# First pair's banks, VectorE order and load order of an attention and expert kernel changed, and the last keys' product as three half-precision passes

## The reference

```
x = x + xattn(layernorm(x), ctx)     # queries from x, keys and values from the context
x = x + attn(layernorm(x))           # 16 heads, rotated queries and keys
x = x + ffn(layernorm(x))            # 8 experts, the best 2 of each token

# xattn, after a second layernorm of the queries and one of the context:
q = x1 @ Wq + bq;  k = x2 @ Wk + bk;  v = x2 @ Wv + bv
attn = softmax(q @ k.T * scaling)    # 32 queries by 257 keys in each batch
y = (attn @ v) @ Wo + bo
```

## Time and profile before

| | |
|---|---|
| median of 3 runs | 574.69 us |
| the profiled execution | 574.39 us |
| its span, first to last instruction | 572.1 us |
| TensorE busy | 488.4 us, 85% |
| VectorE busy | 381.2 us, 67% |
| ScalarE busy | 253.2 us, 44% |
| GpSimd busy | 111.0 us, 19% |
| mean granted TensorE clock | 0.930 |

### The profile page before, as it was taken

The page is one execution under the profiler, slowest core; times in us unless marked ns, Lnnn a source line. Parts: engine busy times, 40 slices in busy tenths (PEclk is TensorE's granted clock), DMA queues, the critical chain, the costliest instruction groups (busy, mean ns, idle before and its releaser), DMA issues.

```text
span 572.1 us, 11023 instructions
## 1 busy us (share of the span) xinstructions
PE 488.4 (85%) x3598; PEld 277.6 (49%) x3599; DVE 381.2 (67%) x850; ACT 253.2 (44%) x392; POOL 111.0 (19%) x88
## 2 busy tenths in 40 slices
PE   4988699998988999859503799999999999999993
PEld 2743266465665777636401344544454445444441
DVE  4776878848979898878785566673655636673230
ACT  1403346465269293948400445652545526542130
POOL 1030122114150222102750011112111211121112
PEclk9979699999999999995655799999999999999998
DMA  8997087920009993361596468787584866734222
GB/s 297 405 391 288 32 340 302 406 103 1 1 2 384 379 383 126 111 220 38 186 320 183 124 198 231 253 233 221 155 255 78 269 168 197 222 77 74 55 55 38
DMA packets 56128, 111.56 MB, mean 195 GB/s; under 512 B 25216, under 2 KB 26272, under 8 KB 50976
## 3 DMA queue, kind: packets, MB, share of 16 engines
q1 hardware_dynamic: 25152, 87.64, 42.2%
q10 hardware_dynamic: 26640, 13.73, 10.0%
q0 software_dynamic: 4304, 9.77, 7.9%
HBM read 76.19 MB, written 29.43 MB: 185 GB/s over the span
## 4 chain that ended last, share of the span: by engine, by line
PE 63%; DVE 15%; DMA 8%; issue 5%; POOL 4%; ACT 2%; SPq 2%; ACTq 0%; POOLq 0%; DVEq 0%
PE bank L716 20%; PE bank L734 19%; PE bank L536 6%; PE bank L355 4%; DMA wbuf<-in_wo 4%; POOL routed_rows L1673 3%; DMA ctx_region<-in_ctx 2%; PE bank L520 2%; PE bank L562 2%; PE bank L427 2%; PE bank L501 2%; PE bank L613 1%; DMA routed_rows<-shared,ints 1%; DVE ctx_region L1324 1%; PE bank L496 1%
## 5 line engine op out<-in xcount | busy, mean ns | idle before, releaser
L716 PE MATMUL bank<-wbuf,ctx_region 128*128 x504 | 116.4, 389 | 6.5 <-issue 5.4
L1458 DVE SCALAR_TENSOR_TENSOR wbuf<-ctx_region,wbuf 128x2048 f32 (+1 forms) x28 | 62.9, 2288 | 32.5 <-ACT wbuf L900 32.5
L1703 POOL DMA_INDIRECT out<-misc,ints x21 | 38.6, 1838 | 229.6 <-ACT misc L981 174.6
L716 PEld LDWEIGHTS bank<-wbuf,ctx_region 128*128 128x128 f16 x504 | 49.0, 100 | 66.0 <-issue 13.9
L900 ACT ACTIVATE wbuf<-ctx_region 128x2048 f32 (+1 forms) x28 | 52.0, 1903 | 29.1 <-issue 29.1
L1608 POOL TENSOR_TENSOR small<-small 128x2 f32<-128x2 f32 (+2 forms) x25 | 27.1, 1088 | 171.4 <-DVE small L1054 160.1
L734 PE MATMUL bank<-wbuf,actT 128*128 x264 | 58.8, 379 | 1.0 <-DVE actT L1568 1.0
L1000 ACT ACTIVATE ctxT_region<-bank 128x512 f32<-128x512 f32 x42 | 25.1, 597 | 67.8 <-PE bank L716 67.8
L734 PE MATMUL bank<-wbuf,xn 128*128 x240 | 53.4, 379 | 0.0
L536 PE MATMUL bank<-ctx_region,wbuf 128*128 128x256 f16 x384 | 43.3, 273 | 3.7 <-DVE ctx_region L1209 3.7
L1562 DVE CAST ctxT_region<-ctxT_region 128x1024 f16<-128x1024 f32 x21 | 14.6, 694 | 42.9 <-ACT ctxT_region L1000 42.9
(11 more groups left out here) (220 smaller groups left out, 790.6 us busy)
## 6 DMA issues: line engine op xcount, KB each, us to landing
ctx_region<-in_experts SPq DMA_DIRECT2D x28, 1024.0 KB
routed_rows<-ctxT_region SPq DMA_DIRECT2D x1, 16900.0 KB, 50.7
ctxT_region<-in_ctxT SPq DMA_DIRECT2D x8, 1542.0 KB, 13.2
ctx_region<-in_ctx SPq DMA_DIRECT2D x8, 1536.0 KB, 10.2
ctx_region<-routed_rows ACTq DMA_DIRECT2D x23, 260.0 KB, 4.0
wbuf<-in_experts SPq DMA_DIRECT2D x4, 1024.0 KB
out<-x ACTq DMA_DIRECT2D x8, 256.0 KB
wbuf<-in_wqT SPq DMA_DIRECT2D x4, 256.0 KB, 7.3
```

What stands on the lines that cost most here:

```text
L716: mm = nc.tensor.matmul(bank[half][:, :], xgT[:, b, x_part, k * P:(k + 1) * P], w16[:, ds(at + (w_part + k * EH + half * 512), 512)], star ...
L1458: nc.vector.scalar_tensor_tensor(w16[:, ds(at + (LOW + n * PIECE), PIECE)], src_[:, piece], W_SCALE, w16[:, ds(at + (HIGH + n * PIECE), PI ...
L1703: nc.gpsimd.indirect_dma_start(out, bass.IndirectOffsetOnAxis(idx[:, slot_no:slot_no + 1].bitcast(U32), axis=0), y_out[:, slot_no, :], Non ...
```

## The change

It has four parts.

1. Banks and waits of pair 0. The third product of `join_values` goes to bank 3 instead of bank 0 and waits for `sc_nb` (tile 1's scores have been read). `join_biases` goes to bank 5 instead of bank 1 and waits for `left_bias` instead of `r_out`. The wait for `m2_lo` moves from between `probs_T` and `queries_T` to ahead of tile 1 of `context_sums`, the wait for `bvo` to ahead of `probs_T`.
2. VectorE's order in pair 0: the first half of `ctx_stats(2)`, `query_second(1)` and `query_shift(1)` now stand ahead of `context_max(0)`, the third `values_low` and `query_stats(2)` behind `probs_scaled(0)`.
3. Load order: `wvT` and `wo` now come ahead of `load_ctx(1)`. At the start the first x tiles come behind `wkT` of block 1, and the semaphores are cut anew, so that `fold(e)` no longer waits for `wqT` of its own block and TensorE's block e waits for `wqT` of its block.
4. The left keys' product is three half-precision passes (high by high, high by low, low by high) behind the other keys, instead of one float32 matmul ahead of them. VectorE makes the two halves of the left rows once (`left16`) and one more half of `p_left` per tile.

```diff
-            sp.dma_start(ln2_rows, t_in["ln2_rows"]).then_inc(s["ln2_in"], 16)
+            sp.dma_start(ln2_rows, t_in["ln2_rows"]).then_inc(qk_in[0], 16)
             for e in range(KC):
                 part = slice(e * P, (e + 1) * P)
                 sp.dma_start(wkT[:, e, :], t_in["wkT"][part, :]).then_inc(qk_in[e], 16)
-                sp.dma_start(wqT[:, e, :], t_in["wqT"][part, :]).then_inc(qk_in[e], 16)
-                if e == 0:
+                if e == 1:
                     sp.dma_start(x_tiles[:, 0:2], x_dram[:, 0:2]).then_inc(s["x_in0"], 16)
+                sp.dma_start(wqT[:, e, :], t_in["wqT"][part, :]).then_inc(qk_in[e + 1], 16)
...
             load_ctxT(1)
-            load_ctx(1)
             sp.dma_start(left_row[0:B, :], t_in["ctx_768"][:, KEYS - 1, :]).then_inc(s["left_in"], 16)
             load_w(wvT, "wvT", s["vo_weights_in"])
             load_w(wo, "wo", s["vo_weights_in"])
+            load_ctx(1)
...
-                pe.wait_ge(qk_in[e], 32)
+                pe.wait_ge(qk_in[e + 1], 32 if e + 1 < KC else 16)
...
                         join_biases()
+                        pe.wait_ge(s["sc_nb"], 2)
                     for e in range(KC):
-                        mm = nc.tensor.matmul(bank[(6, 7, 0)[k]][:, :], wvT[:, e, k * P:(k + 1) * P], wo[:, e, :],
+                        mm = nc.tensor.matmul(bank[(6, 7, 3)[k]][:, :], wvT[:, e, k * P:(k + 1) * P], wo[:, e, :],
                                               start=(e == 0), stop=(e == KC - 1))
...
-                pe.wait_ge(s["r_out"], 2)
+                pe.wait_ge(s["left_bias"], 3)
...
-                    pe.wait_ge(s["pT"], 2 * tile + 2)
-                    nc.tensor.matmul(bank[2 + t][:, 0:DC], p_left[0:B, t, :], left_row[0:B, :], start=True, stop=False,
-                                     skip_group_check=True)
+                    pe.wait_ge(s["pT"], 3 * tile + 1)
+                    if tile == 1:
+                        pe.wait_ge(s["m2_lo"], CC)
...
+                    pe.wait_ge(s["pT"], 3 * tile + 3)
+                    for p_part, x_part in PASSES:
+                        mm = nc.tensor.matmul(bank[2 + t][:, 0:DC], p_left[0:B, p_part, t, :], left16[0:B, x_part, :],
+                                              start=False, stop=(p_part == 1), skip_group_check=True)
                     mm.then_inc(s["cv_ps"], 1)
...
+                if pair == 0:
+                    pe.wait_ge(s["bvo"], 1)
                 probs_T(pair)
-                if pair == 0:
-                    pe.wait_ge(s["m2_lo"], CC)
-                    pe.wait_ge(s["bvo"], 1)
...
-                    nc.vector.tensor_scalar(p_left[0:B, t, :], bank[4 + t][0:B, 2 * P:3 * P], l_rstd[0:B, :], None, ALU.mult)\
+                    nc.vector.tensor_scalar(p_left[0:B, 0, t, :], bank[4 + t][0:B, 2 * P:3 * P], l_rstd[0:B, :], None, ALU.mult)\
                         .then_inc(s["pT"], 1)
+                    dve.wait_ge(s["pT"], 3 * tile + 2)
+                    nc.vector.scalar_tensor_tensor(p_left[0:B, 1, t, :], bank[4 + t][0:B, 2 * P:3 * P], l_rstd[0:B, :],
+                                                   p_left[0:B, 0, t, :], ALU.mult, ALU.subtract).then_inc(s["pT"], 1)
...
+            left = left_row[0:B, :]
+            count(nc.vector.tensor_copy(left16[0:B, 0, :], left), "norm_step")
+            count(nc.vector.tensor_tensor(left16[0:B, 1, :], left, left16[0:B, 0, :], ALU.subtract), "norm_step", wait=False)
             query_stats(1)
+            ctx_stats(2, (0,))
+            query_second(1)
+            query_shift(1)
```

More of the change, by code:

```diff
@@ L66 @@
 ROWS_W = 2 * D + E
-SEMS = """const_in x_in0 x_in1 x_in left_in qk_in0 qk_in1 qk_in2 qk_in3 vo_weights_in self_qk_in self_vo_in
-rows_in cols_in ln2_in ctxT_in0 ctxT_in1
+SEMS = """const_in x_in0 x_in1 x_in left_in qk_in0 qk_in1 qk_in2 qk_in3 qk_in4 vo_weights_in self_qk_in self_vo_in
+rows_in cols_in ctxT_in0 ctxT_in1
 ctx_in0 ctx_in1 ctx_in2 ctx_in3
@@ L92, in program @@
         ctx_in = (s["ctx_in0"], s["ctx_in1"], s["ctx_in2"], s["ctx_in3"])
-        qk_in = (s["qk_in0"], s["qk_in1"], s["qk_in2"], s["qk_in3"])
+        qk_in = (s["qk_in0"], s["qk_in1"], s["qk_in2"], s["qk_in3"], s["qk_in4"])
         ctxT_in = (s["ctxT_in0"], s["ctxT_in1"])
@@ L177, in program @@
         pT = c.take(2, 2 * P)
-        p_left = c.take(2, P)
+        p_left = c.take(2 * P).bitcast(F16).rearrange("p (a t q) -> p a t q", a=2, t=2)
         left_row = c.take(DC)
@@ L182, in program @@
         ln2_rows = actT[:, 0:KW + DC]
+        left16 = actT[:, 0:DC].bitcast(F16).rearrange("p (a d) -> p a d", a=2)
         ln2_b_row, ln2_g_row = actT[:, 0:KW], actT[:, KW:KW + DC]
@@ L433, in join_biases @@
                 pe.wait_ge(s["bv_step"], KC + 1)
-                pe.wait_ge(s["r_out"], 2)
+                pe.wait_ge(s["left_bias"], 3)
                 for e in range(KC):
-                    mm = nc.tensor.matmul(bank[1][:, :], bv_total[:, e:e + 1].to_broadcast([P, P]), wo[:, e, :],
+                    mm = nc.tensor.matmul(bank[5][:, :], bv_total[:, e:e + 1].to_broadcast([P, P]), wo[:, e, :],
                                           start=(e == 0), stop=(e == KC - 1))
@@ L500, in context_sums @@
                             at = c2 * P + b * L
-                            mm = nc.tensor.matmul(bank[2 + t][b * L:(b + 1) * L, 0:DC], pT[:, t, at:at + L],
-                                                  ctx_n[:, tile % 4, b, c2, :], start=False, stop=(c2 == 1),
-                                                  tile_position=(0, b * L), skip_group_check=True)
+                            nc.tensor.matmul(bank[2 + t][b * L:(b + 1) * L, 0:DC], pT[:, t, at:at + L],
+                                             ctx_n[:, tile % 4, b, c2, :], start=(c2 == 0), stop=False,
+                                             tile_position=(0, b * L), skip_group_check=True)
+                    pe.wait_ge(s["pT"], 3 * tile + 3)
+                    for p_part, x_part in PASSES:
+                        mm = nc.tensor.matmul(bank[2 + t][:, 0:DC], p_left[0:B, p_part, t, :], left16[0:B, x_part, :],
+                                              start=False, stop=(p_part == 1), skip_group_check=True)
                     mm.then_inc(s["cv_ps"], 1)
@@ L841, in _ @@
                         act.wait_ge(s["m2_ps"], k + 1)
-                        nc.scalar.activation(m2[:, 0, k, :], bank[(6, 7, 0)[k]][:, :], ACT.Copy, scale=ln2_g_scaled[:, k:k + 1])\
+                        nc.scalar.activation(m2[:, 0, k, :], bank[(6, 7, 3)[k]][:, :], ACT.Copy, scale=ln2_g_scaled[:, k:k + 1])\
                             .then_inc(s["m2_hi"], 1)
@@ L1134, in values_low @@
                 dve.wait_ge(s["m2_hi"], k + 1)
-                nc.vector.scalar_tensor_tensor(m2[:, 1, k, :], bank[(6, 7, 0)[k]][:, :], ln2_g_scaled[:, k:k + 1], m2[:, 0, k, :],
+                nc.vector.scalar_tensor_tensor(m2[:, 1, k, :], bank[(6, 7, 3)[k]][:, :], ln2_g_scaled[:, k:k + 1], m2[:, 0, k, :],
                                                ALU.mult, ALU.subtract).then_inc(s["m2_lo"], 1)
@@ L1260, in _ @@
                 if pair == 0:
-                    query_second(1)
-                    query_shift(1)
-                    ctx_stats(2, (0,))
-                    values_low(0)
+                    ctx_stats(2, (1,))
                     dve.wait_ge(s["rows_in"], 32)
@@ L1267, in _ @@
                     bo = row("bo")[0:64, :]
-                    nc.vector.tensor_tensor(bo, bank[1][0:64, :], bo, ALU.add).then_inc(s["bvo"], 1)
+                    nc.vector.tensor_tensor(bo, bank[5][0:64, :], bo, ALU.add).then_inc(s["bvo"], 1)
+                    values_low(0)
+                    values_low(1)
                     dve.wait_ge(s["bvo"], 1)
@@ L1273, in _ @@
                                                    ALU.mult, ALU.subtract).then_inc(s["bvo"], 1)
-                    values_low(1)
-                    ctx_stats(2, (1,))
-                    query_stats(2)
-                    values_low(2)
                 if pair:
@@ L1284, in _ @@
                 probs_scaled(pair)
+                if pair == 0:
+                    values_low(2)
+                    query_stats(2)
                 if pair + 1 < PAIRS:
```

1 line of the change is left out of this document (removed).

## The result

The kernel after has a median of 574.92 us (573.34 to 578.38, 22 runs), the kernel before 572.83 us (566.88 to 576.36, 22 runs). The ratio is 1.0055, 95% interval 1.0036 to 1.0074: 0.55% slower, 2.1 to 4.2 us. The forecast was 570.7 us, range 567.0 to 574.0. The result lies outside it, on the other side of no change.

What follows compares the result with a forecast made beforehand. TensorE, slowed by the load of `wo`, leads until 46.40 us, then VectorE. A 2.5 us loss to the first maximum is included in 3.9 gained at pair 1, then 3.4, 3.6, 3.7: 574.4 - 3.7 = 570.7 us, range 567.0 to 574.0.

Steps and rivals of the forecast that it cites:

- Tile 1 and the first maximum: Start to VectorE's first maximum: tile 1 lands at 34.9, maximum at 48.9 instead of 46.40, a 2.5 us loss.
- From the first maximum to pair 1: VectorE, 48.9 to 75.8 us against 33.3 us before; pair 1 begins 3.9 us earlier, the 2.5 loss included.
- the wait ahead of `asked(1)`: TensorE before pair 1: a 2.8 us wait from 62.8 to 65.6 replaces the one of 7.17 us.
- The second rival: TensorE's clock falls in the new gap before `asked(1)`: price 1.5 us, 572.3 us in all; chance 0.14.
- The passes: Left keys' product: three passes take 0.51 us against 0.88, saving TensorE 0.37 us a tile if it leads.
- The step that failed: Pair 3: TensorE saves 1.0 us, VectorE's new work uses 0.7 of 0.80 slack, 0.1 kept; nothing changes behind.
- a late tile 1: Start, tile 1's load: landing at 38.6 uses up the gain, at 42.1 gives 578 us; chance 0.07.

Runs made afterwards that it cites:

- e1: Kernel after, with GpSimd's clearing of `k_exp` put behind pair 0's normalisation: 569.0 us, ratio to before 0.9942.
- e4: Kernel after without part 4, the float32 product of the left keys back: 568.73 us, ratio to before 0.9915.
- e2: Kernel before, with GpSimd's clearing of `k_exp` let go one tile of context sums earlier: 576.5 us, ratio 1.0055.
- e3: Kernel before with part 4, the half-precision passes, alone: 576.89 us, ratio 1.0071.
- e9: Kernel after, both GpSimd clearings put behind VectorE's normalisations and tile 1's context load back in its old place: 567.64 us, ratio to before 0.9893.
- e5: Kernel after, with two of `k_exp`'s four blocks cleared at the old place, the others behind the normalisation: 573.04 us, ratio to before 0.999.
- e10: Repeat of e8's kernel (after without passes, both clearings waiting, tile 1's load in its old place): 564.44 us, ratio to before 0.9843.
- e6: Kernel before, with both GpSimd clearings (`k_exp`, `p_T`) put behind their normalisations: 573.37 us, ratio 0.9997.
- e8: Kernel after without passes, both clearings behind their normalisations, tile 1's context load back in its old place: 566.23 us, ratio to before 0.9866.

## Why the prediction failed, point by point

**Tile 1 and the first maximum.** The waits came as forecast. `ctx_stats(1)` waited for its load until 34.0 (34.9 forecast), TensorE's second product for `q_bias` until 39.93 (40.8), the clock fell in that gap (5.40 us for the product, between the 3.70 it took in e1 and e4 and the 6.8 assumed; the earlier trace rows has 8 records in 6.18 us at 1.2 GHz, so 6.8 was too much even for the low clock), and the maximum came at 47.63 (48.9). Of the two engines that the forecast had arrive together, VectorE alone set it: 13.6 us of work from its start at 34.03, as forecast (48.5 - 34.9), while TensorE's product was done at 45.33. The forecast called this a loss of 2.5 us against 46.40, and by the two profiles it is 1.2. But the base was the error: the profile before was a late execution of its load order. Its `join_values` took 10.20 us for two products, at 1.2 GHz for the first 6.2 us. In e2 and e3, with the same loads, the two products took 7.13. From mean to mean of the two orders (table) the loss is 3.0. That it came close to 2.5 is partly luck, a maximum forecast 1.3 us too late against a base 2.3 us above its mean. The windows showed the low clock, and nothing in one execution shows that it is not always there.

**From the first maximum to pair 1.** Forecast 75.8 - 48.9 = 26.9 us against 33.3. Measured 74.53 - 47.63 = 26.90. Each step held: `ctx_stats(4)` at 69.96 (71.2 forecast, from a start 1.3 later) without a wait for its load, the wait ahead of `asked(1)` 2.48 (2.8). The second rival's mechanism came too: `asked(1)` took 5.77 us instead of 4.10 behind that wait, with a granted clock of 0.76 in 64 to 71 us (1.00 in e1). It cost nothing here, since VectorE, with `ctx_stats(4)`, led to 74.53. The forecast had given it 1.5 us. The same wait left the clock up in e1 and e9 (4.11 and 4.10 us) and brought 6.98 us in e5, where pair 1's first L523 came 1.2 us later.

**The passes.** From start to start of the next matmul three passes take 0.58 us (0.51 forecast), as in these rows of after:

```profile
125.56 0.66 PE L508 MATMUL bank<-actT,misc 32*128 32x384 f16 x3
126.14 1.50 PE L503 MATMUL bank<-ctx_region,misc 128*32 128x384 f32 x16
```

The float32 matmul took 0.84 us in most tiles of the kernel before, and 0.88 in the row that the forecast used. So the passes save 0.26 us a tile and not 0.37. The Trainium skill, page "FP8 and Floating Point Precision", section "TensorE Precision Notes", has float32 as four passes; an estimate from it, three quarters of 0.88, would be 0.66. The measurement lies between that and my figure, and nothing in the time hangs on it. VectorE's new half took 0.34 us each, 0.7 a pair as forecast. What was wrong is that anything is left of the saving. From the first maximum to L523 the passes cost about 1.3 us in the changed kernel: 90.36 against 89.09 in e9 and e10, 90.34 against 89.01 in e1 and e4. The medians do not tell it from nothing. Most of it lies in pair 0: from the maximum to pair 1 e9 needs 26.89 us and e10 25.79 (69.42 and 69.02 from 42.53 and 43.23), and all four kernels with the passes take 26.88 to 26.90, the four without them 25.79 to 25.81.

In the order of the kernel before the passes gain instead: e3 takes 31.98 us from the maximum to pair 1, the others with this order 33.26 to 33.35. There the load of tile 4 is waited for (1.20 us in e2, nothing in e3), and it is let go by the end of tile 0's sums, which the passes shorten. Of the gain 0.9 us is left against e2 ahead of pair 3. The price of the passes thus has another sign in another order.

**The step that failed.** "Pair 3: TensorE saves 1.0 with the wait for `p_left` [...] 0.1 is kept: 3.7", and behind it "Behind that nothing is changed, and no load or fill there is tied to an absolute time." I asked what TensorE's earlier end and VectorE's later one do to each other, with 0.80 us of slack between them, and not what else hangs on them. GpSimd's clearing hangs on the one, and the normalisation on the other. Before, the last sums ended 1.6 us after the normalisation began (134.0 and 132.36), and the normalisation takes 1.0. The passes, which stand behind the other keys, and the 0.7 us more on VectorE brought the two to within 0.2 us (128.2 and 128.05). No load is tied to an absolute time, but a fill was tied to another engine's.

The price: 3.3 us of holding, and 1.7 of clock behind the wait that it makes. The first part is shown by its dose. The second stands in all four executions with the collision, but also in one of the eight without it (e8), so the hold makes it likely, as far as twelve executions tell, but is not needed for it. The table has 5.0 between e1 and after, the medians 1.13% of 572.8, 6.5, and the two intervals leave 4.0 to 9.0. At L523 the forecast had the kernel 3.7 us earlier and the table has it 1.7 later; the collision is 5.0 of these 5.4. That the kernel before had a collision of 4.15 us in plain sight, at 141.20 us, is a row I had not read. e6 shows that it costs nothing there, which is also why its line is no warning by its price.

By the Trainium skill, page "SBUF — State Buffer", section "Who interferes with whom", VectorE's `tensor_scalar` from and to SBUF can take both port pairs, of which one is GpSimd's, and whoever issues first has the pair for the whole instruction while the other "**fully blocks**". The traces agree. The hold goes with the length of GpSimd's instruction, 3.27 us more with 3.75 and 1.57 more with 2.05, and the `scalar_tensor_tensor` on the weights does not feel the clearing beside it. That it is the ports, and nothing else that the two engines share, no run here shows. I had not applied that page to a change that moves no instruction of either kind. That is the reading it asks for.

**Forecast and result together.** Without the collision (e1) the kernel is 3.3 us faster than the kernel before, where the forecast had 3.7. Up to the first maximum it loses 3.0 us by the table (forecast 2.5), and from there to L523 it gains 6.4 (forecast 2.5 + 3.7 = 6.2). Its 569.0 us lie 1.7 below the forecast mainly because the kernel before measured 572.24 beside it, and the forecast counted from 574.39. With the collision the time is 574.92, 4.2 above the forecast. No rival named GpSimd. The one on the other side, a late tile 1, did not happen.

**What stays open.** Behind 143 us to the start of the third big expert product (TensorE's L721, L716 before, at 336.54 before and 338.98 after) the executions take 193.2 to 196.2 us. Before took 193.4, after 196.0, but e10 and e4, without a collision, took 196.2 and 195.4, and e3, with one, 194.1. What differs there in the traces is at which matmuls the granted clock is low: in 240 to 250 us it was 0.83 in the four kernels that had 0.66 in 130 to 140, and 0.91 to 1.00 in the others. Rows of this stretch, TensorE of after and of before:

```profile
244.24 2.53 PE L619 MATMUL bank<-wbuf,actT 128*128 128x512 f16 x8 [2.83 <-DVE small L1405]
246.56 1.91 PE L623 MATMUL bank<-wbuf,actT 128*128 128x512 f16 x4
```

```profile
244.43 1.89 PE L613 MATMUL bank<-wbuf,actT 128*128 128x512 f16 x8 [2.84 <-DVE small L1394]
246.16 1.03 PE L617 MATMUL bank<-wbuf,actT 128*128 128x512 f16 x4
```

That link held in all twelve executions, but the length of the whole stretch does not follow it, so I charge none of the loss to it. Nor do I know why after took 2.6 us longer than before in it. What remains between the 5.0 us of the table and the 6.5 of the medians may lie there or in the spread of the runs. Also open is what decides whether the clock falls ahead of the 48 matmuls: it fell in e5, with waits of 0.42, 1.37 and 1.35 us from the normalisation on, and not in e1, with 0.42 and 1.85; it fell in e8 and not in e10, with the same 0.51 and 1.25.

## What to carry to other kernels

When an engine ends earlier, list what its semaphores release on the engines that are idle, fills and clearings too, and look at which instruction of VectorE will be running then: a GpSimd clearing of 3.5 us that is free beside one form holds another for nearly its whole length. A fill that nobody needs yet can be put behind the instruction that it would hold, for one wait. And read the start of the trace in more than one execution before pricing a load order, since one profile can mislead: here before's lay 2.3 us above the mean of its load order at the first maximum, and e9's whole execution (564.06) 3.6 us below its median.

## What the runs showed of the hardware that I had not expected

- VectorE's two `tensor_scalar` (128x512 float32, SBUF to SBUF), 1.00 us alone, take 4.15 to 4.28 us beside a GpSimd clearing of 3.51 to 3.76 us and 2.57 beside one of 2.05. The clearing itself is 0.2 us longer where VectorE was first (3.75 and 3.76 us, starting 0.24 behind VectorE, against 3.51).
- The hold of 3.3 us cost 5 us, as TensorE's clock fell behind it: 7.16 us instead of 5.42 for the same 48 matmuls. With the hold halved they took 7.14. One execution without any hold (e8) took 7.08.
- The kernel before and its three variants with the same load order (e2, e3, e6) reached the first maximum between 41.8 and 46.4 us, with 7.13 to 10.20 us for the same 16 records of `join_values`. That spread is wider than the whole effect of the change.
